# A graph layer and routed experts in one program: eight segment masks held, loads of x moved behind the edge rows, the last group's ranks and lists moved forward

## The chip, the cores and the metric

The kernel runs on one core of a Trainium2 chip. The time is device time in microseconds (us) of one execution. TensorE is PE, VectorE is DVE, ScalarE is ACT, GpSimd is POOL, SyncE is SP. "Line" is a line of the kernel before the change.

## The reference

`x` has 10000 rows of 1024 numbers (float32), and there are 5000 edges `src`, `dst`, sorted by `dst`.

```python
# 1: graph layer
h  = layernorm(x) * rsqrt(mean(square(.)) + 1e-6) * rms_w @ W_down     # 10000 x 256
xl, xr = (h @ Wl), (h @ Wr)                                            # 4 heads of 64
msg = xl[src] + xr[dst]          # edges, and one loop per row
e   = einsum(leaky(msg, 0.2), att)                                      # per head
p   = exp(e - segment_max(e, dst)[dst])
out = segment_sum(p / (segment_sum(p, dst)[dst] + 1e-16) * xl[src], dst)
x   = x + out @ W_up
# 2: experts, on xn = layernorm(x)
topk = top_k(xn @ expert_tokens.T, 2)                                   # of 8 experts
for i in range(8):
    w = mean(topk == i); y = gelu(gelu(xn @ W1[i] + b1[i]) @ W2[i] + b2[i]) @ W3[i] + b3[i]
    out2 += y * w
x = x + out2
```

A row that no edge ends in has only its loop, so its aggregate is its own `xl`; only rows that an edge ends in need the segment sums.

## The kernel before

**Engines and order.** Every engine has its own written-out program. Semaphores tie them together; nothing plans the order, it's the order of the code. SP and ACT issue plain transfers, each in its own queue, POOL the indirect ones. An issue takes the issuing engine's program time, and what stands behind it on that engine waits.

**Stage A** (0 to 403 us): 20 groups of 500 rows (125 partitions x 4 rows, `ax`). PE transposes x and multiplies by the centred `W_down` with a high and a low part of each number (`turn`, `down`), DVE makes the low parts (`low`, line 1001) and the row statistics (`bn_a`, line 973; `moments_a`), ACT the high parts. Before that, DVE scales `W_down` by `rms_w` (line 1024, 8 pieces, semaphore `wd_sums`), PE sums it over the rows (line 1650), DVE takes the mean off (line 1032), makes the low part (1040), and copies the expert tokens (`tok_c`, line 1042). Tables of `xl` and of own rows go to `node_table`.

**Stage B** (414 to 549): gathers of both ends of the edges, messages, scores, the segment maxima.

**The edge rows** (549 to 621). The edges are 40 chunks of 125, taken 4 at a time: 10 batches. DVE weighs the messages (line 1261), PE sums a carry over the chunks (line 1750), and DVE copies it (lines 1279, 1281); SP puts it as one more row below `xls` (line 449). A batch (`segment_sums`, line 1762) multiplies the weighted messages by a mask `smat` (126 x 500: same segment or not, line 1271, DVE). `finish` (lines 1284 to 1301, DVE) adds the row's own part (1293), takes the reciprocal, and scales (1299). SP stores the batch (line 455). Two masks are held: the mask of batch b + 2 is made inside `finish(b)`. The middle eight batches run in a hardware loop (`Fori`), the first and the last two are written out. ACT meanwhile weighs the own rows, and issues loads of x for the first groups of stage C (`load_cx`, line 870: 112 and 13 partitions, 2 MB together): groups 0 and 1 when the carry is copied, group 2 when the last mask is made, groups 3 to 5 when the first gather of stage C has landed.

**Stage C** (621 to 956), 20 groups: POOL gathers the aggregate (`gather_rows`, line 657), PE transposes it (line 1777), ACT splits it (`split_agg`, line 892), PE makes routing scores (1788) and eight pieces of the up projection (lines 1570 to 1572), DVE adds each to x (`residual`, 1331), takes statistics (`bn_c`), ranks the experts, and gives each row its place in a list per pair of experts: `ranks_in` and `ranks_past` on PE, `place`, `slots`, `slot_numbers` on DVE (lines 1392 to 1402), `enlist` on POOL (line 674). SP stores x1 (line 472). Six buffers `cx` hold x; from group 6 on, a load waits until the group that had its buffer is stored. For a group, ranks are counted in the group after it. For the last one they come at its end, behind the second half of its moments.

**The turn to stage R** (950 to 975): DVE computes a table of tiles from the counts (lines 1459 to 1492), SP waits for that and for all list entries, and loads lists (line 492); POOL gathers rows by them (line 714). Stage R runs 66 tiles of 256 rows, bound to a pair of experts each.

Of the kernel before, what the change touches and what calls it, by code (L numbers as in the profile page):

```python
# [23 lines left out]
HID, H = 256, 4  # L24
HD = HID // H
NE, EH = 8, 64
P, J = 125, 4
G = P * J
NG = N // G
# [8 lines left out]
CB = 4  # L38
# [17 lines left out]
NX, NI, AHEAD = 8, 16, 5  # L56
NCX = 6
NR, N3 = 4, 4
# [19 lines left out]
def build(nc, x, src, dst, rms_w, w_down, wl, wr, att, w_up, tok, w1, b1, w2, b2, w3, b3, out):  # L78
    ctx = ExitStack()
    with ctx:  # L80
# [6 lines left out]
        def run_of(at, *items):  # L87

            made = []
            for name, shape, dt in items:  # L90
                made.append(put(name, shape, dt, at))
                size = 2 if dt == BF16 else 4
                for n in shape[1:]:
                    size *= n
                at += (size + 31) // 32 * 32
            return (*made, at)

        def sem(name):
# [103 lines left out]
        tot, rden, lsb, carry, sums_end = run_of(  # L202
            at4,
            ("tot", [P, CB, H], F32), ("rden", [P, CB, H], F32), ("lsb", [NC, HV], F32), ("carry", [NC, HV], F32))
        smat, smat_end = run_of(at_wr, ("smat", [P + 1, 2, CB, P], F32))
        assert smat_end <= at_wr + 2 * KH * HID * 4

# [15 lines left out]
        xn = [xn0, xn1]  # L223
        assert c_end <= at4 - J * ROW * 4 and sums_end <= at_cx1 and edges_end + NI * NS * 4 <= at0 and xn_end <= at0, (c_end, at_cx0, edges_end, xn_end, at0)
        assert origin + max(late_end, b_end, r_end) <= nc.sbuf_usable_end, (a_end, b_end, r_end, nc.sbuf_usable_end - origin)
# [314 lines left out]
        def _(pool):  # L540
# [126 lines left out]

            def enlist(g):

                pool.wait_ge(c_slot, g + 1)  # L670
                if g == 0:
                    pool.wait_ge(sent_put, 16 * ((PAIRS + 1) * CAP // (128 * SENT)))
                for j in range(J):
                    pool.indirect_dma_start(
                        out=lists[:, :], out_offset=bass.IndirectOffsetOnAxis(ap=slot[:, g % 2, j:j + 1], axis=0),
                        in_=tok_id[:, g, j:j + 1], in_offset=None).then_inc(list_put[g % 2], 16)
# [11 lines left out]
            for g in range(NG):  # L688
# [6 lines left out]
                if g == S0 + 1:  # L695
                    lower_w2_table()
            rstd_c(NG - 1, slice(0, J // 2), NG)
            rstd_c(NG - 1, slice(J // 2, J), NG + 1)
            enlist(NG - 1)

# [47 lines left out]
        def _(act):  # L749
# [126 lines left out]
            load_cx(0)  # L876
            load_cx(1)
            with act.Fori(6, NB) as b:
                weigh_own(b)
            act.wait_ge(b_sb, NB)  # L880
            load_cx(2)
            act.wait_ge(rows_stored, 32 * NB)
            act.wait_ge(agg_loaded[0], 16 * J)
            for g in range(3, NCX):
                load_cx(g)

# [6 lines left out]

            split_agg(0)
            for g in range(NG):
                if g + 1 < NG:
                    split_agg(g + 1)
                if 2 <= g and g + NCX - 2 < NG:
                    act.wait_ge(x1_put[(g - 2) % 3], 32 * ((g - 2) // 3 + 1))
                    load_cx(g + NCX - 2)  # L900
                if g == S0:
                    act.wait_ge(raw_w2, 16 * 2)
                    act.activation(w2_tab[:, :, 0:EH], w2_raw[:, :, EH:2 * EH], ACT.Copy).then_inc(w2_hi, 1)
# [65 lines left out]
        def _(dve):  # L969
# [53 lines left out]
            for k in range(KD):  # L1023
                last = dve.tensor_scalar(wdx[:, k, 0:HID], wd_raw[:, k, :], rmsw[:, k:k + 1], None, ALU.mult)
            last.then_inc(wd_sums, 1)
            low(0)
            low(1)
            dve.wait_ge(tok_split, 1)
            dve.wait_ge(wd_sums, 2)
            for half in range(2):  # L1030
# [4 lines left out]
            for half in range(2):  # L1035
# [5 lines left out]
                                  ).then_inc(wd_ready, 1)  # L1041
            dve.tensor_copy(tok_c[:, :, :], wdx[:, :, HID:HID + NE]).then_inc(setup_v, 2)
            for piece in range(8):
                bn_a(0, piece)
# [76 lines left out]
            for i in range(NROW):  # L1121
# [18 lines left out]
                if j == J - 1 and 0 <= g - GS1 < KD:  # L1140
                    low_w1(g - GS1)
                if i == J + 1:
                    dve.wait_ge(raw_idx, 16 * 9)
                    dve.tensor_copy(idx_f[:, :, :], idx_rows[:, :, :]).then_inc(setup_v, 1)
# [122 lines left out]

            def same_segment(b, par):

                wait(dve, b_num, b - 1)  # L1270
                dve.tensor_tensor(smat[:, par, :, :],
                                  dst_row[:, bass.ds(CB * P * b, CB * P)].rearrange("p (c e) -> p c e", c=CB),
                                  dst_col[:, bass.ds(CB * b, CB)].unsqueeze(2).broadcast_to([P + 1, CB, P]),
                                  ALU.is_equal).then_inc(b_sb, 1)

            same_segment(0, 0)
            same_segment(1, 1)
            dve.wait_ge(b_l, 1)
# [4 lines left out]
            def finish(b, par):  # L1283
# [11 lines left out]
                dve.reciprocal(rden[:, :, :], tot[:, :, :]).then_inc(b_den, 1)  # L1295
                if has_batch(b, 2):
                    same_segment(b + 2, par)
                dve.wait_ge(b_den, 3 * b + 3)
                dve.tensor_tensor(by_head, by_head, rden[:, :, :].unsqueeze(3).broadcast_to([P, CB, H, HD]),
                                  ALU.mult).then_inc(b_out, 1)  # L1300

            def has_batch(b, more):
                return not isinstance(b, int) or b + more < NB

# [101 lines left out]
            for g in range(NG):  # L1406
# [35 lines left out]
                if not more:  # L1442
                    bias_c(g, slice(0, J // 2), NG)
                for u in range(6, 8):
                    residual(g, u)
                    bn_c(g, u)
                if more:
                    moments(g, g % 2, c_bn, c_aggr, c_var, 1.0, LN_EPS)
            moments(NG - 1, (NG - 1) % 2, c_bn, c_aggr, c_var, 1.0, LN_EPS, J // 2, J, 1)
            place(NG - 1)  # L1450
            slots(NG - 1)
            bias_c(NG - 1, slice(J // 2, J), NG + 1)
            slot_numbers(NG - 1)

# [112 lines left out]
        def _(pe):  # L1567
# [79 lines left out]
            pe.wait_ge(tok_split, 1)  # L1647
            pe.wait_ge(wd_sums, 1)
            for k in range(KD):
                last = pe.matmul(X_A[1][:, 0:HID + NE], ones_raw[:, :], wdx[:, k, :], start=k == 0, stop=k == KD - 1,  # L1650
                                 skip_group_check=True)
# [106 lines left out]
            def segment_sums(b, par):  # L1758
                pe.wait_ge(b_sb, b + 1)
                wait(pe, b_out, b - 1)  # L1760
                for q in range(CB):
                    last = pe.matmul(bank[4 * par + q][0:P, 0:HV], smat[:, par, q, :],
                                     xls[0:P + 1, bass.ds(CB * b + q, 1), :].rearrange("p c d -> p (c d)"),
                                     start=True, stop=True, skip_group_check=True)
                last.then_inc(b_num, 1)
# [64 lines left out]
            for g in range(NG):  # L1830
# [11 lines left out]
                if g >= 1:  # L1842
                    ranks_past(g - 1)
                for u in range(6, 8):
                    up(g, u)
            ranks_in(NG - 1)
            ranks_past(NG - 1)
# [92 lines left out]
```

## Time and profile before

| | us |
|---|---|
| three runs: median, lowest, highest | 1629.34, 1626.74, 1630.38 |
| the profiled execution's own time | 1625.11 |
| its span | 1623.4 |
| PE busy | 1486.6 (92%) |
| DVE busy | 1189.4 (73%) |
| ACT busy | 687.3 (42%) |
| POOL busy | 653.3 (40%) |

The span runs from the first to the last instruction of the profiled execution. Times of the rows further down are microseconds from its start. Busy time is a union over a stretch and can be high on several engines at once; a "<-" behind an idle time names what ended it. For a DMA the row is the issue, the landing comes later. In a row of a merged group, "x8" is the number of instructions and the length is that of the whole group.

### The profile page before, as it was taken

The numbers are of one execution on the slowest core, as the hardware profiler recorded it, in microseconds if no ns is written. First come the engines' busy times: TensorE is split into PE (matmuls) and PEld (weight loads), VectorE is DVE, ScalarE is ACT, GpSimd is POOL, SyncE is SP. The second block draws the span as 40 slices with busy tenths as digits, with TensorE's granted clock in tenths as the row PEclk, the third lists the DMA queues.
The fourth block names the chain that finished last, engine by engine and source line by source line (L and its number), as shares of the span: only waits on it lengthen the run. The fifth ranks groups of instructions, "written<-read, shape, count | busy, mean of one in ns | idle before, by whom it ended". The sixth has DMA issues, their size and how long they took to land.

```text
span 1623.4 us, 28905 instructions
## 1 busy us (share of the span) xinstructions
PE 1486.6 (92%) x9321; PEld 1234.1 (76%) x9321; DVE 1189.4 (73%) x2415; ACT 687.3 (42%) x1365; POOL 653.3 (40%) x729
## 2 busy tenths in 40 slices
PE   6999999999599654999999938999999999999997
PEld 5999999999477433888877837777777777777775
DVE  5666666667297763999999956777777777777775
ACT  2444445544244540000000005666666666566653
POOL 2112222223676002576666553444444444444432
PEclk9999999999799886999999968999999999999999
DMA  8887876552464078899999567767666666665320
GB/s 202 231 194 184 174 199 156 156 150 65 126 187 154 1 191 223 211 315 293 310 303 294 186 169 206 220 220 219 219 206 202 215 211 210 213 207 165 106 57 15
DMA packets 121662, 306.95 MB, mean 189 GB/s; under 512 B 63855, under 2 KB 65557, under 8 KB 114015
## 3 DMA queue, kind: packets, MB, share of 16 engines
q1 hardware_dynamic: 60088, 155.40, 34.8%
q0 software_dynamic: 50848, 108.78, 21.2%
q10 hardware_dynamic: 10580, 40.96, 9.8%
q8 instruction: 75, 1.23, 0.3%
q14 instruction: 71, 0.58, 0.1%
HBM read 220.40 MB, written 138.85 MB: 221 GB/s over the span
## 4 chain that ended last, share of the span: by engine, by line
PE 46%; issue 21%; DVE 17%; POOL 7%; DMA 5%; SPq 1%; ACTq 0%; POOLq 0%; DVEq 0%; ACT 0%
PE psum L1894 14%; PE psum L1862 7%; PE psum L1570 6%; PE psum L1572 5%; PE psum L1571 5%; DVE stat L973 5%; DVE cx L1331 4%; PE psum L1892 4%; POOL where_from L606 2%; POOL xls L639 1%; DVE aggt_lo L1321 1%; POOL td L643 1%; POOL rstd L595 1%; PE psum L1750 1%; DMA agg<-node_table,from_idx 1%
## 5 line engine op out<-in xcount | busy, mean ns | idle before, releaser
L1894 PE MATMUL psum<-w_raw,gl 128*128 128x512 f32 x528 | 269.7, 592 | 0.0
L917 ACT ACTIVATE xt_hi<-psum 128x512 fp32r<-128x512 f32 x264 | 151.0, 598 | 240.0 <-PE psum L1862 239.9
L1498 DVE TENSOR_TENSOR xt_lo<-psum,xt_hi 128x512 fp32r<-128x512 f32 x264 | 176.4, 689 | 87.4 <-ACT xt_hi L917 86.7
L1511 DVE SCALAR_TENSOR_TENSOR xb<-psum,xb 128x512 f32<-128x512 f32 x264 | 176.1, 687 | 28.7 <-PE psum L1894 28.6
L1609 PE MATMUL psum<-wdx_hi,axt_hi 128*125 128x272 f32 x640 | 190.7, 298 | 6.8 <-DVE wd_lo L1040 4.0
L1001 DVE TENSOR_TENSOR axt_lo<-psum,axt_hi 128x500 fp32r<-128x500 f32 x160 | 108.4, 678 | 118.2 <-ACT axt_hi L754 118.2
L1862 PEld LDWEIGHTS psum<-ident,xn 128*128 128x128 f32 x1056 | 127.1, 142 | 86.0 <-issue 68.4
L1611 PE MATMUL psum<-wdx_hi,axt_lo 128*125 128x272 f32 x640 | 184.9, 289 | 0.0
L1610 PE MATMUL psum<-wd_lo,axt_hi 128*125 128x256 f32 x640 | 179.7, 281 | 0.0
L726 POOL DMA_INDIRECT out<-xb,idx_in x132 | 134.0, 1015 | 106.2 <-issue 59.7
L911 ACT ACTIVATE xn<-xb 128x1024 f32<-128x1024 f32 x132 | 156.1, 1233 | 45.1 <-DMA xb<-rows_x,idx_in 45.1
L1570 PE MATMUL psum<-xt_hi,st_w 128*128 128x256 f32 x528 | 167.4, 317 | 0.0
L1862 PE MATMUL psum<-ident,xn 128*128 128x128 f32 x1056 | 150.3, 276 | 17.4 <-ACT xn L911 16.9
L714 POOL DMA_INDIRECT xb<-rows_x,idx_in x132 | 141.4, 1071 | 59.4 <-issue 54.7
L1892 PE MATMUL psum<-b_hl,sel_st 128*128 128x512 f32 x264 | 158.8, 601 | 0.0
L1572 PE MATMUL psum<-xt_hi,st_w 128*128 128x256 f32 x528 | 150.5, 285 | 0.0
L892 ACT ACTIVATE aggt_hi<-psum 128x500 fp32r<-128x500 f32 x40 | 21.4, 586 | 304.9 <-PE psum L1777 262.1
L1571 PE MATMUL psum<-xt_lo,st_w 128*128 128x256 f32 x528 | 150.1, 284 | 0.0
L754 ACT ACTIVATE axt_hi<-psum 128x500 fp32r<-128x500 f32 x160 | 94.3, 590 | 123.5 <-PE psum L1593 123.4
L1894 PEld LDWEIGHTS psum<-w_raw,gl 128*128 128x128 f32 x528 | 99.9, 189 | 44.1 <-issue 32.1
L1570 PE MATMUL psum<-wup_hi,aggt_hi 128*125 128x512 f32 x320 | 132.8, 415 | 0.0
L595 POOL TENSOR_TENSOR rstd<-var,neg_half 125x4 f32<-125x4 f32 x20 | 23.8, 1192 | 266.9 <-DVE var L983 266.9
(276 smaller groups left out, 3841.4 us busy)
## 6 DMA issues: line engine op xcount, KB each, us to landing
w_raw<-in_L_ffn_W SPq DMA_DIRECT2D x140, 256.0 KB, 12.5
cx<-in_x ACTq DMA_DIRECT2D x20, 1792.0 KB
rows_x<-cx SPq DMA_DIRECT2D x19, 1806.0 KB
ax<-in_x SPq DMA_DIRECT2D x19, 1792.0 KB
node_table<-trow SPq DMA_DIRECT2D x19, 896.0 KB
node_table<-xld SPq DMA_DIRECT2D x10, 448.0 KB
cx<-in_x ACTq DMA_DIRECT2D x20, 208.0 KB
rows_x<-cx SPq DMA_DIRECT2D x19, 209.6 KB
```

Source lines behind the costliest of these rows:

```text
L911: act.activation(xn[s][:, :], xb[:, b, s, 0:D], ACT.Identity, bias=xb[:, b, s, D + 1:D + 2], scale=xb[:, b, s, D:D + 1]).then_inc(r_xn, 1)
L1498: dve.tensor_tensor(xt_lo[:, 2 * q:2 * q + 2, :].rearrange("p k n -> p (k n)"), T_R[q % 2], xt_hi[:, 2 * q:2 * q + 2, :].rearrange("p k n ...
L1511: dve.scalar_tensor_tensor(piece, Y[u], 0.5, piece, ALU.mult, ALU.add).then_inc(r_res, 1)
L1570: pe.matmul(out_ap, left[0], right[0], start=start, stop=False, skip_group_check=True)
L1571: pe.matmul(out_ap, left[0], right[1], start=False, stop=False, skip_group_check=True)
L1572: return pe.matmul(out_ap, left[1], right[0], start=False, stop=stop, skip_group_check=True)
L1609: pe.matmul(into, high, wdx_hi[:, k, :], start=k == 0, stop=False, skip_group_check=True)
L1610: pe.matmul(into[:, 0:HID], high, wd_lo[:, k, :], start=False, stop=False, skip_group_check=True)
L1611: last = pe.matmul(into, low, wdx_hi[:, k, :], start=False, stop=k == KD - 1, skip_group_check=True)
L1862: last = pe.transpose(T_R[q % 2][:, TT * k + 128 * s:TT * k + 128 * (s + 1)], xn[s][:, 128 * (2 * q + k):128 * (2 * q + k + 1)], ident[:, :])
L1892: pe.matmul(Y[u], sel_st[:, t % 2, :], b3_hl[:, HALF * n:HALF * (n + 1)], start=True, stop=False, skip_group_check=True)
L1894: pe.matmul(Y[u], gl2[:, t % 2, rows], w3_raw[:, t % N3, HALF * n:HALF * (n + 1)], start=False, stop=True, skip_group_check=True).then_inc ...
```

## The change

- `smat` holds eight masks (`NSM`) in place of two. It moves to the place that the small sums had, and these to the place of the masks. Eight masks are made before the carry's copy; `finish` makes one only in the written-out batches 0 and 1 (for 8 and 9).
- `load_cx`: group 0 as before, group 1 when the edge rows are stored and the first gather has landed, groups 2 to 5 behind the first `split_agg`.
- Start: the wait for the scaled weights is split in two (`wd_sums`); four of eight statistics pieces of group 0 stand ahead of the wait for the sums; the copy `tok_c` moves to the fifth row step of stage A.
- Last group: PE counts the ranks between its up pieces 6 and 7, DVE makes the slots ahead of residuals 6 and 7, POOL issues two list entries ahead of the last power and two behind.

```diff
-NCX = 6
+NCX, NSM = 6, 8
...
-            at4,
+            at_wr,
             ("tot", [P, CB, H], F32), ("rden", [P, CB, H], F32), ("lsb", [NC, HV], F32), ("carry", [NC, HV], F32))
-        smat, smat_end = run_of(at_wr, ("smat", [P + 1, 2, CB, P], F32))
+        smat, smat_end = run_of(at4, ("smat", [P + 1, NSM, CB, P], F32))
...
-            def enlist(g):
+            def enlist(g, first=0, past=J):
...
-                for j in range(J):
+                for j in range(first, past):
...
             rstd_c(NG - 1, slice(0, J // 2), NG)
+            enlist(NG - 1, 0, J // 2)
             rstd_c(NG - 1, slice(J // 2, J), NG + 1)
-            enlist(NG - 1)
+            enlist(NG - 1, J // 2, J)
...
             load_cx(0)
-            load_cx(1)
             with act.Fori(6, NB) as b:
                 weigh_own(b)
-            act.wait_ge(b_sb, NB)
-            load_cx(2)
             act.wait_ge(rows_stored, 32 * NB)
             act.wait_ge(agg_loaded[0], 16 * J)
-            for g in range(3, NCX):
-                load_cx(g)
+            load_cx(1)
...
             split_agg(0)
+            for g in range(2, NCX):
+                load_cx(g)
...
-            last.then_inc(wd_sums, 1)
+                if k % (KD // 2) == KD // 2 - 1:
+                    last.then_inc(wd_sums, 1)
             low(0)
             low(1)
+            for piece in range(4):
+                bn_a(0, piece)
             dve.wait_ge(tok_split, 1)
-            dve.wait_ge(wd_sums, 2)
+            dve.wait_ge(wd_sums, 3)
...
-            dve.tensor_copy(tok_c[:, :, :], wdx[:, :, HID:HID + NE]).then_inc(setup_v, 2)
-            for piece in range(8):
+            for piece in range(4, 8):
                 bn_a(0, piece)
...
+                if i == J:
+                    dve.tensor_copy(tok_c[:, :, :], wdx[:, :, HID:HID + NE]).then_inc(setup_v, 2)
...
-            same_segment(0, 0)
-            same_segment(1, 1)
+            for b in range(NSM):
+                same_segment(b)
...
-                if has_batch(b, 2):
-                    same_segment(b + 2, par)
+                if isinstance(b, int) and b + NSM < NB:
+                    same_segment(b + NSM)
...
                 if not more:
                     bias_c(g, slice(0, J // 2), NG)
+                if not more:
+                    place(g)
+                    slots(g)
+                    slot_numbers(g)
...
             moments(NG - 1, (NG - 1) % 2, c_bn, c_aggr, c_var, 1.0, LN_EPS, J // 2, J, 1)
-            place(NG - 1)
-            slots(NG - 1)
             bias_c(NG - 1, slice(J // 2, J), NG + 1)
-            slot_numbers(NG - 1)
...
-            pe.wait_ge(wd_sums, 1)
             for k in range(KD):
+                if k % (KD // 2) == 0:
+                    pe.wait_ge(wd_sums, 2 * k // KD + 1)
...
-                for u in range(6, 8):
-                    up(g, u)
-            ranks_in(NG - 1)
+                if g == NG - 1:
+                    up(g, 6)
+                    ranks_in(g)
+                    up(g, 7)
+                else:
+                    for u in range(6, 8):
+                        up(g, u)
             ranks_past(NG - 1)
```

## Rows read from the trace of the kernel before

**Rows 1.** Busy time by stretch: engine busy (count), granted PE clock, DMA share, GB/s.

```profile
60.00:500.00 440.00, 417.13 (x3366) 401.27 (x3366) 288.00 (x639) 199.78 (x433) 140.60 (x161) 0.98 0.64 163
...
640.00:660.00 20.00, 20.00 (x97) 16.49 (x96) 16.80 (x39) 1.07 (x2) 2.17 (x2) 0.93 1.00 221
...
700.00:1050.00 350.00, 316.03 (x1695) 258.20 (x1694) 301.03 (x717) 66.14 (x111) 198.30 (x195) 0.94 0.84 253
...
1100.00:1600.00 500.00, 500.00 (x2872) 375.64 (x2871) 374.11 (x629) 307.92 (x524) 213.84 (x247) 1.00 0.59 180
```

**Rows 2.** Timeline of the start: start, length, what, idle time before.

```profile
11.77 5.11 PE L1650 MATMUL psum<-wdx,ones_raw 128*128 128x264 f32 x16
...
17.00 2.42 DVE L1032 SCALAR_TENSOR_TENSOR wdx<-psum,wdx 128x1056 f32<-128x1056 f32 x2 [3.69 <-PE psum L1650]
...
21.90 1.27 DVE L1042 COPY tok_c<-wdx 128x64 f32<-128x64 f32 x1
...
23.09 4.83 DVE L973 BATCH_NORM_STATS2 stat<-ax 125x6 f32<-125x512 f32 x8
...
25.89 0.59 PE L1593 MATMUL psum<-ident,ax 125*128 125x125 f32 x4
...
29.33 0.39 PE L1609 MATMUL psum<-wdx_hi,axt_hi 128*125 128x272 f32 x1 [2.84 <-DVE axt_lo L1001]
```

**Rows 3.** Timeline of the edge rows, DVE, and PE's first batch.

```profile
570.22 0.42 DVE L1279 COPY lsb<-psum 40x260 f32<-40x260 f32 x1 [7.83 <-PE psum L1750]
...
590.15 0.17 DVE L1290 SCALAR_TENSOR_TENSOR tot<-psum,pexp 125x16 f32<-125x16 f32 x1
...
591.53 0.62 DVE L1271 TENSOR_TENSOR smat<-dst_row,dst_col 126x500 f32 x1
...
593.19 0.17 DVE L1290 SCALAR_TENSOR_TENSOR tot<-psum,pexp 125x16 f32<-125x16 f32 x1
...
608.39 0.17 DVE L1290 SCALAR_TENSOR_TENSOR tot<-psum,pexp 125x16 f32<-125x16 f32 x1
...
611.04 0.17 DVE L1290 SCALAR_TENSOR_TENSOR tot<-psum,pexp 125x16 f32<-125x16 f32 x1
...
580.20 5.93 PE L1762 MATMUL psum<-xls,smat 126*125 126x260 f32 x16 [8.87 <-DMA xls<-carry]
```

**Rows 4.** Chain at the last store; DMA busy strip of 595 to 605.

```profile
614.50 6.51 DMA node_table<-xld
...
DMA  9986310008999876200006999888300009999988
```

**Rows 5.** Chain and ACT timeline at the start of stage C.

```profile
629.97 0.62 ACTq L870
...
634.02 0.60 ACT aggt_hi L892
...
647.13 1.07 ACT L892 ACTIVATE aggt_hi<-psum 128x500 fp32r<-128x500 f32 x2 [12.04 <-PE psum L1777]
```

**Rows 6.** SyncE's DMA issues at 13 to 14 us.

```profile
13.11 7.83 SPq L411 DMA_DIRECT2D b_raw<-in_L_ffn_b  x1
```

**Rows 7.** Gathers of stage C (line 657), and PE's waits of 640 to 945.

```profile
DMA to landing us min/median/max: 2.8/8.9/15.0
...
PE psum L1777 <- DMA agg<-node_table,from_idx: 3.9, 4, 1.7
```

**Rows 8.** Timeline of the last group: DVE, then POOL, then SyncE.

```profile
949.09 0.42 DVE L1392 TENSOR_TENSOR steps<-psum,onehot 125x256 f32<-125x256 f32 x1
...
950.56 0.23 DVE L1459 TENSOR_TENSOR beats<-psum,bcap 125x64 f32<-125x64 f32 x1 [0.32 <-PE psum L1806]
...
955.27 0.42 DVE L1492 CAST tile_tab<-psum 1x264 int32<-1x264 f32 x1 [1.09 <-PE psum L1852]
...
955.70 1.18 POOL L674 DMA_INDIRECT lists<-tok_id,slot  x1 [0.30 <-issue]
...
959.31 4.75 SPq L492 DMA_DIRECT2D idx_in<-lists  x5
```

More of the change, by code:

```diff
@@ L202, in build @@
         tot, rden, lsb, carry, sums_end = run_of(
-            at4,
+            at_wr,
             ("tot", [P, CB, H], F32), ("rden", [P, CB, H], F32), ("lsb", [NC, HV], F32), ("carry", [NC, HV], F32))
-        smat, smat_end = run_of(at_wr, ("smat", [P + 1, 2, CB, P], F32))
-        assert smat_end <= at_wr + 2 * KH * HID * 4
+        smat, smat_end = run_of(at4, ("smat", [P + 1, NSM, CB, P], F32))
+        assert sums_end <= at_wr + 2 * KH * HID * 4
         cx3, cx4, agg, aggt_hi, aggt_lo, cx5, c_end = run_of(
@@ L223, in build @@
         xn = [xn0, xn1]
-        assert c_end <= at4 - J * ROW * 4 and sums_end <= at_cx1 and edges_end + NI * NS * 4 <= at0 and xn_end <= at0, (c_end, at_cx0, edges_end, xn_end, at0)
+        assert c_end <= at4 - J * ROW * 4 and smat_end <= at_cx0 and edges_end + NI * NS * 4 <= at0 and xn_end <= at0, (c_end, at_cx0, edges_end, xn_end, at0)
         assert origin + max(late_end, b_end, r_end) <= nc.sbuf_usable_end, (a_end, b_end, r_end, nc.sbuf_usable_end - origin)
@@ L1266, in _, with same_segment @@
                 weigh(b)
[L1268 to L1273, printed above, removed]
+            def same_segment(b):
+                dve.tensor_tensor(smat[:, b % NSM, :, :],
+                                  dst_row[:, CB * P * b:CB * P * (b + 1)].rearrange("p (c e) -> p c e", c=CB),
+                                  dst_col[:, CB * b:CB * (b + 1)].unsqueeze(2).broadcast_to([P + 1, CB, P]),
                                   ALU.is_equal).then_inc(b_sb, 1)
-            same_segment(0, 0)
-            same_segment(1, 1)
+            for b in range(NSM):
+                same_segment(b)
             dve.wait_ge(b_l, 1)
@@ L1300, in finish @@
                                   ALU.mult).then_inc(b_out, 1)
-            def has_batch(b, more):
-                return not isinstance(b, int) or b + more < NB
             for par in range(2):
@@ L1761, in segment_sums @@
                 for q in range(CB):
-                    last = pe.matmul(bank[4 * par + q][0:P, 0:HV], smat[:, par, q, :],
+                    last = pe.matmul(bank[4 * par + q][0:P, 0:HV], smat[:, b % NSM, q, :],
                                      xls[0:P + 1, bass.ds(CB * b + q, 1), :].rearrange("p c d -> p (c d)"),
```

## The prediction

> **What bounds the kernel now.** Every term below is measured against the profiled execution, whose own time is 1625.1 us around a span of 1623.4 us (the table of times above); the median of the three timed runs is 1629.3, which is 4.2 us above it. I read the table of stretches first, then the timeline at the two ends of each stage, then the chain of waits.
>
> The stretches [rows 1] show two long stages in which TensorE (PE) does the work and one in which it shares the bound. The first stage (normalise and project all rows, "stage A") keeps PE at 417 of 440 us, and most of what is missing there lies at its far end. The last one (the experts, "stage R") keeps PE at 500 of 500. Between 700 and 1050, mostly the 20 row groups of "stage C" (aggregate, up projection, residual, routing), VectorE (DVE) is busy for 301 us and PE for 316 of 350. The change touches none of the loops of A and R in number or kind of instruction. So it can only move the joints: the first 30 us, the edge rows at 584 to 634, and the turn from C to R at 945 to 960. The order of work inside a long stage is fixed, and whatever a joint gives is carried to the end, unless the next stage waits for something that didn't move.
>
> **1. The start.** PE goes through the sums over the weights without a wait before them: that row has no idle time noted [rows 2]. The new split of the wait (first half, then all) therefore removes nothing: 0, and bounded by 0 on both sides within rounding.
>
> Moving the first four statistics pieces of group 0 ahead of the wait for those sums is another matter. DVE stands idle for 3.69 us until 17.00 for PE's sums; four pieces cost 4 x 0.60 = 2.4 us (4.83 us for eight) and fit in, if their rows have landed. The rows of that group are loaded in four parts in order, PE has used the first by 12, and there is room of 1.3 us. Behind the centred weights, DVE now runs the copy of the tokens (21.90, 1.27 us; its next instruction starts 1.19 later), eight pieces (4.83 us), then the moments, and only then the low part for which PE waits: 2.84 us idle until 29.33 [rows 2]. Without the copy and with four pieces fewer, DVE reaches that low part 1.2 + 2.4 = 3.6 us earlier, at 25.0. PE itself ends its transposes only at 26.48 (25.89 + 0.59), so of the 3.6 no more than the 2.84 of idle time can go: the next step of PE starts at about 26.4. What is late next is the load of group 1: DVE's first piece of it stood behind the low part, at 29.2, and now comes at about 26; by the order and size of the loads it may have to wait until 27.5, which puts the second low part some 0.4 us behind its old distance. I take **2.5 us**, between 0 (the load of group 1 sets the pace anyway) and 2.84.
>
> The copy of the tokens comes back later in stage A (1.27 us, once), where DVE has 152 of 440 us free [rows 1] and PE is fed from four buffers: 0, at most 1.3 if it hits a low part directly.
>
> **2. The edge rows.** Ten batches run on DVE one after the other. A batch with a mask made inside takes 3.04 us (590.15 to 593.19), the last one, which makes none, 2.65 (608.39 to 611.04) [rows 3]. Now eight masks are made ahead, and only batches 0 and 1 still make one (for 8 and 9), so batches 2 to 7 go from 3.04 to 2.65: 6 x 0.39 = **2.3 us**. The six additional masks, of 0.62 us each, lie before the copy at 570.22, ahead of which DVE idles 7.83 us: 3.7 us of masks are hidden, with 4 to spare. What could be late next is PE: it needs 2.0 us for a batch's sums and may begin one when DVE has finished two batches before, so it has 2.65 us and is still hidden by some 0.4. Bounds: 0 (PE or the register arithmetic of the loop is exposed) to 6 x 0.62 = 3.7, the whole mask.
>
> **3. The last stores of the edge rows.** Before the gathers of stage C may start, all stores must have landed. The last one takes 6.51 us from its issue [rows 4], because the load of x for group 2 was released by the last mask at 607 and lies in front and among the stores. With nothing beside them, stores show as separate bursts in the strip of 595 to 605 (a digit is 0.25 us): issued every 3.04 us, the bursts end some 2.9 us behind the issue and the queues fall idle between them. The change moves that load behind the gathers, so the last store should take about 3.0: **3.5 us**, between 0 and 3.9. The earlier load of group 1 is moved too. It ended beside the first stores, with no wait depending on it, 0. The load of group 0 is still issued beside the carry row, so PE's wait of 8.87 us for that row [rows 3] stays; I give the missing second load nothing there, since it queued behind the first (bounds 0 to 4).
>
> **4. ScalarE's issues ahead of the first high part.** When the first gather has landed, ScalarE (ACT) issues six halves of loads, then splits the aggregate: the third issue starts at 629.97 and the split at 634.02 [rows 5]. Now only the load of group 1 (two issues) stands there. So the split starts where the third issue did: **4.0 us**. The other eight issues come behind the split. They take 0.6 to 0.9 us each, 6 to 8 us together, and behind them waits the split of group 1. That was due 13.1 us after the first (647.13), with 12.04 us idle before it [rows 5]: cover for 5 to 6 us more.
>
> This is the weakest place. Never were more than three loads (6 MB) in flight on ACT's queue; now it's five, 10 MB. And on SyncE's queue, one issue took 7.83 us in place of 0.3 to 0.4 when much was in flight [rows 6]. The Trainium skill, page "DMA: Bandwidth & Descriptors", section "Anatomy of one DMA", says of GpSimd's path that descriptor generation is a small part of a transfer's fixed cost and that many can be emitted before it shows; by that rule the eight issues stay cheap and the sum stands, by the row just named they may not.
>
> Do the loads come in time? Loads alone run at 221 GB/s (640 to 660, DMA share 1.00 [rows 1]), so 2 MB take 9.3 us. Group 1's x lands some 10 us behind the split and is used 24 behind it; those of 2 to 5 land by 22, 31, 40 and 50 and are used at 39, 54, 70 and 85. No residual waits for x.
>
> **5. The last group.** Now the ranks of group 19 are counted and turned into slots ahead of its residuals 6 and 7, and the first half of the list entries goes out before the last moments. Three small DVE steps (0.42, 0.42, 0.17 with their waits: 1.1 us, [rows 8]) move ahead of the last two residuals, so those, the second moments, the last bias (949.99) and the last store come 1.1 us later; the count of tiles starts 0.65 later than 950.56, since it no longer follows the slots but the bias. The tile table is then written at 955.9 instead of 955.27, done by 956.4. On GpSimd (POOL), the last four list issues, 1.49 us apart, end with the one at 955.70; its landing, about 2.6 us later at 958.3, lets SyncE read two numbers and issue the first list at 959.31, 1.0 behind [rows 8]. Two of the four now run at 947 to 950, beside the residuals; the two others start behind the second power at 951.2, the last at 952.7, so that they land 2.5 us later at 955.3. The gate is no longer the lists but the tile table at 956.4, against 958.3: **1.9 us**, between 0 (the stores of x1, later by 1.1, become the gate) and 2.9 (the lists alone).
>
> **Sum:** 2.5 + 2.3 + 3.5 + 4.0 + 1.9 = 14.2 us. The profiled execution would go from 1625.1 to 1610.9, the median of runs from 1629.3 to **1615**.
>
> **The rivals.**
>
> *ACT's queue holds no more than three loads.* For it speaks the 7.83 us issue [rows 6]; against it, that the six issues at 628 to 634 show no such wait, and that SyncE's slow one was of another shape. Price: the fourth load is let in when group 1's has landed and the fifth when group 2's has, about 22 us behind the first split (two loads of 9.3 us and the gathers between them). The split of group 1, due at 13, is 9 us late, and with it PE and DVE. Gain 14.2 - 9 = 5: **1624**.
>
> *The start gives nothing that lasts.* The load of group 1, or the table's and the map's stores between A and the gathers at 414, set the pace and not PE. The map's last writes follow a power of DVE's last moments, which PE paces, which speaks against. Gain 11.7: **1617.6**.
>
> *DMA is the bound of stage C.* Two loads, 4.1 MB, are moved from the edge rows, where the queues were partly idle, into the stage where the DMA share is 0.84 on average at 253 GB/s [rows 1]. If nothing there is spare, they cost 4.1 / 0.253 = 16 us and eat the rest: **1631**, no change. Against it: DVE waits in C for no load, only for PE.
>
> *The gathers come late (the other side, slower).* A gather of a group lands 2.8 to 15.0 us behind its issue, median 8.9, and is used about 15 us after it; PE already waits for it four times, 3.9 us in all, 1.7 at most [rows 7]. With more loads queued for longer, the gathers of groups 3 to 19 would each come 1.7 us late and DVE, the bound, would follow: 17 x 1.7 = 29 us, **1644**. It decides from 14.2 / 17 = 0.84 us per group. The Trainium skill, same page, section "Queues, rings and completion order", says that an engine goes round-robin between its queues packet by packet; by that a longer queue of loads takes no more from the gathers than a short one that is never empty. In the rows, the share stays high through C before the change too, which agrees but doesn't settle the first 40 us.
>
> **How the numbers follow.** Forecast 0.62, ACT's queue 0.18, start lost 0.09, DMA bound 0.05, gathers late 0.06. A difference under 0.2% (3.3 us) can't be told from none. Faster: the forecast, the lost start, and three quarters of the queue's case (it gains 5, less if the wait is longer): 0.84. Same: the rest of that case and the DMA bound, 0.09. Slower: 0.07. For the range: all upper bounds together, 2.84 + 3.7 + 3.9 + 4 (carry row) + 4.0 + 2.9 = 21.3, would give 1608, which is unlikely as a whole; the low end is 1610. The high end takes in the queue's case: 1625.
>
> **What would show it.** In the profile after: PE's wait at 29.33 gone and its step at 26.4 to 27; tot instructions 2.65 us apart from the third batch on; the first gather of stage C 6 us closer to the first batch; the first split of the aggregate 1.5 us behind the first gather's landing and not 5.6; the eight issues behind it under 1 us each, and the second split still 13 us after the first; groups of C still 15.3 us apart; the first list read about 2 us closer to the last residual. It would be wrong if an issue among the eight takes several us, if residuals wait for x, or if stage C takes longer than before from its first split to its last.

## The result and the profile after

| | before, us | after, us |
|---|---|---|
| median of 12 runs each | 1627.99 | 1622.32 |
| lowest, highest | 1621.65, 1634.11 | 1615.82, 1624.68 |
| profiled execution: own time, span | 1625.11, 1623.4 | 1623.03, 1621.3 |

The ratio is 0.996, with a 95% interval of 0.9944 to 0.9977. The change makes the kernel faster by 0.4%, 5.7 us by the medians. Forecast were 14.2 us and a time of 1615; the measured one lies in the range (1610 to 1625) only by its upper part, which had been drawn for the rival "ACT's queue holds no more than three loads" (1624). The gain itself is less than half of the one forecast.

The stretches of the kernel after come first, in the columns of [rows 1] (the five busy times are those of PE, PE's weight loads, DVE, ACT and POOL):

```profile
60.00:500.00 440.00, 417.21 (x3358) 400.38 (x3358) 288.91 (x641) 199.22 (x434) 142.72 (x162) 0.98 0.65 164
640.00:660.00 20.00, 11.54 (x44) 9.65 (x43) 9.96 (x26) 1.06 (x2) 4.93 (x5) 0.66 1.04 215
700.00:1050.00 350.00, 313.85 (x1695) 255.39 (x1696) 301.34 (x717) 66.35 (x111) 197.54 (x196) 0.95 0.85 254
1100.00:1600.00 500.00, 500.00 (x2876) 375.84 (x2875) 374.68 (x628) 306.93 (x523) 214.01 (x247) 1.00 0.58 179
```

The long stages are as they were. The odd row is the second: PE worked for 20 of the 20 us before [rows 1], and now for 11.54, with the DMA share still full. That hole is new, and the timeline of ScalarE and its queue shows what made it (start, length, what, idle time before and its cause; ACTq is ACT issuing a DMA):

```profile
619.78 1.62 ACTq L871 DMA_DIRECT2D cx<-in_x  x2
621.45 0.59 ACT L889 ACTIVATE aggt_hi<-psum 128x500 fp32r<-128x500 f32 x1 [33.86 <-PE psum L1778]
...
623.67 3.36 ACTq L871 DMA_DIRECT2D cx<-in_x  x1
...
628.17 8.62 ACTq L871 DMA_DIRECT2D cx<-in_x  x1
...
638.48 7.83 ACTq L871 DMA_DIRECT2D cx<-in_x  x1
...
646.37 1.06 ACT L889 ACTIVATE aggt_hi<-psum 128x500 fp32r<-128x500 f32 x2 [23.85 <-issue]
```

The first split stands at 621.45, where it was 634.02 [rows 5]. Then come the eight issues. Three of them don't take 0.6 to 0.9 us but 3.36, 8.62 and 7.83 (all three are the second, small issue of a load, that of 13 partitions), and the second split waits behind them: "23.85 <-issue" says that it waited for nothing but its own engine's issues. It starts 24.92 us after the first; before, the distance was 13.11 [rows 5]. The first split had been 12.57 us sooner than before; of these, 11.81 are gone at the second. DVE and PE pass the wait on (their rows at the second group):

```profile
646.99 0.68 DVE L1320 TENSOR_TENSOR aggt_lo<-psum,aggt_hi 128x500 fp32r<-128x500 f32 x1 [8.77 <-ACT aggt_hi L889]
...
649.24 0.38 PE L1789 MATMUL psum<-m,aggt_hi 128*125 128x16 f32 x1 [8.46 <-DVE aggt_lo L1320]
```

Both traces cut at the same landmarks give the account. "C" is stage C, and "last scaling" is the end of DVE's last one.

| from, to | before | after | gained |
|---|---|---|---|
| start to first gather of stage B | 414.59 | 413.42 | 1.17 |
| to PE's first edge sums | 165.61 | 164.19 | 1.42 |
| first edge sums to last scaling | 33.57 | 31.15 | 2.42 |
| last scaling to first gather of C | 8.02 | 4.11 | 3.91 |
| first gather to first split | 12.24 | 8.59 | 3.65 |
| first split to second split | 13.11 | 24.92 | -11.81 |
| second to last (20th) split | 275.75 | 277.38 | -1.63 |
| last split to first list load | 36.35 | 35.00 | 1.35 |
| first list load to end | 664.17 | 662.55 | 1.62 |
| sum (the spans) | 1623.41 | 1621.31 | 2.10 |

How far can such a row be read? The same landmarks in the nine profiles of before, after and the versions below (all but e4) say it. The second row took 163.4 to 168.0 us and the seventh 275.8 to 279.3 (once 283.6), with the same instructions in them. The first row is 414.4 to 415.0 in the three with the old start, but 412.2 to 416.1 in the six with the new one. The last row took 662.1 to 664.4. So 1.17, 1.42, -1.63 and 1.62 are no findings of their own. The rows from the edge sums to the first split repeat to 0.6 us at most.

The rows at the start, to be set against [rows 2]:

```profile
11.81 5.89 PE L1651 MATMUL psum<-wdx,ones_raw 128*128 128x264 f32 x16
17.82 2.42 DVE L1034 SCALAR_TENSOR_TENSOR wdx<-psum,wdx 128x1056 f32<-128x1056 f32 x2 [2.09 <-PE psum L1651]
...
22.71 2.47 DVE L972 BATCH_NORM_STATS2 stat<-ax 125x6 f32<-125x512 f32 x4
25.32 0.42 DVE L979 BATCH_NORM_AGGREGATE mv<-stat 125x2 f32<-125x12 f32 x4
25.78 0.17 DVE L982 TENSOR_SCALAR var<-mv 125x4 f32<-125x4 f32 x1
25.86 0.67 DVE L1000 TENSOR_TENSOR axt_lo<-psum,axt_hi 128x500 fp32r<-128x500 f32 x1
27.18 0.69 DVE L972 BATCH_NORM_STATS2 stat<-ax 125x6 f32<-125x512 f32 x1 [0.65 <-DMA ax<-in_x]
```

Only four pieces are left behind the weights (2.47 us, 4.83 before), and DVE's low part comes at 25.86 instead of 28.60. The last row is what is late next, as forecast: the load of group 1. One thing ate into the gain in this execution: PE's weight sums ended 0.8 later (17.70, against 16.88), and all behind them with it.

The edge rows (DVE; against [rows 3]) and the last store (against [rows 4]):

```profile
558.83 4.79 DVE L1273 TENSOR_TENSOR smat<-dst_row,dst_col 126x500 f32<-126x500 int32 x8
568.17 0.42 DVE L1281 COPY lsb<-psum 40x260 f32<-40x260 f32 x1 [4.54 <-PE psum L1751]
...
577.60 6.32 PE L1763 MATMUL psum<-xls,smat 126*125 126x260 f32 x16 [8.33 <-DMA xls<-carry]
...
587.56 0.17 DVE L1292 SCALAR_TENSOR_TENSOR tot<-psum,pexp 125x16 f32<-125x16 f32 x1
...
590.20 0.17 DVE L1292 SCALAR_TENSOR_TENSOR tot<-psum,pexp 125x16 f32<-125x16 f32 x1
...
607.53 1.23 DVE L1301 TENSOR_TENSOR xld<-xld,rden 125x1024 f32<-125x1024 f32 x1
612.15 0.24 DVE L1315 MEMSET cx<- 125x24 f32 x6 [3.40 <-DMA node_table<-xld]
612.86 0.95 POOL L657 DMA_INDIRECT agg<-node_table,from_idx  x1 [91.30 <-DMA node_table<-xld]
```

Eight masks take 4.79 us ahead of the copy, and DVE still idles 4.54 before it. Batches are 2.64 apart from the third on. DVE waits 3.40 us for the last store.

The last group (DVE, POOL, SyncE; against [rows 8]):

```profile
945.96 0.14 DVE L1340 SCALAR_TENSOR_TENSOR cx<-mv,cx 125x2 f32<-125x2 f32 x1
946.02 0.41 DVE L1391 TENSOR_TENSOR steps<-psum,onehot 125x256 f32<-125x256 f32 x1
...
948.03 1.24 POOL L674 DMA_INDIRECT lists<-tok_id,slot  x1 [3.55 <-DVE slot L1401]
...
953.32 1.18 POOL L674 DMA_INDIRECT lists<-tok_id,slot  x1 [0.30 <-issue]
956.02 0.42 DVE L1492 CAST tile_tab<-psum 1x264 int32<-1x264 f32 x1 [1.08 <-PE psum L1857]
957.53 0.48 DVE L1533 MEMSET st_w<- 128x512 f32 x1 [1.09 <-DMA rows_x<-cx]
...
958.84 2.60 SPq L492 DMA_DIRECT2D idx_in<-lists  x3
```

The order is the new one. The forecast's times were on the clock of the profile before, where the last split stands at 922.88; here it stands at 923.75, so distances from it are what can be compared. The tile table comes 32.3 us behind it (32.4 before, 33.0 forecast) and the last list entry goes out 29.6 behind it (29.8 forecast). But the first list is read 35.0 behind it by the table above and not 34.5 as forecast (36.35 before): the last list entry went out at 953.32 and took 4.44 us to land,

```profile
953.32 4.44 DMA lists<-tok_id,slot
```

beside the last store of x1, which DVE's row at 957.53 also waits for. In all seven profiles with the new order that entry takes 4.1 to 4.4 us and goes out 1.2 us behind the last store of x1; in the three with the old order it takes 2.5 to 2.6 and goes out 5.2 behind. The gate stayed the lists.

### The profile page after: what moved, and what is told of

It is laid out like the page before. It is cut to its first block and busy times, and to the rows that moved or that the text cites. A ratio compares the mean times of both kernels' runs of the same rounds, so it can differ in the third digit from the quotient of the medians.

```text
span 1621.3 us, 28896 instructions
## 1 busy us (share of the span) xinstructions
PE 1488.0 (92%) x9321; PEld 1234.7 (76%) x9321; DVE 1189.9 (73%) x2415; ACT 686.2 (42%) x1365; POOL 653.3 (40%) x729
## 3 DMA queue, kind: packets, MB, share of 16 engines
q10 hardware_dynamic: 10580, 40.96, 10.0%
```

## The experiments

All are ratios to the kernel before, run on the same chip, with 95% intervals. The question of the first four: do the long issues take back what the moved loads give (theory Q), or is DMA the bound of stage C (rival D), and what are the start and the last group worth alone?

**e1_spread.** The kernel after, with two loads behind the first split and one behind each of the next two, instead of four behind the first:

```diff
-            for g in range(2, NCX):
+            for g in range(2, NCX - 2):
                 load_cx(g)
 ...
-                if 2 <= g and g + NCX - 2 < NG:
-                    act.wait_ge(x1_put[(g - 2) % 3], 32 * ((g - 2) // 3 + 1))
+                if g + NCX - 2 < NG:
+                    if g >= 2:
+                        act.wait_ge(x1_put[(g - 2) % 3], 32 * ((g - 2) // 3 + 1))
                     load_cx(g + NCX - 2)
```

> The changed kernel, but only the loads of groups 2 and 3 stand behind the first split; the load of group 4 is issued behind the second split and that of group 5 behind the third. Rival D (stage C pays for the moved bytes anyway, the blocked issue is only where it shows): the second split is early, but the groups behind it are late by as much, and the ratio stays near 0.996.

Measured: 1613.47 us (before 1626.27), ratio 0.9926, 0.99 to 0.9952; repeated as e8_spread_again below: 1612.34, ratio 0.9914, 0.9891 to 0.9936. ACT in the first of them:

```profile
620.19 0.59 ACT L889 ACTIVATE aggt_hi<-psum 128x500 fp32r<-128x500 f32 x1 [34.30 <-PE psum L1779]
...
622.41 2.61 ACTq L871 DMA_DIRECT2D cx<-in_x  x1
633.33 0.59 ACT L889 ACTIVATE aggt_hi<-psum 128x500 fp32r<-128x500 f32 x1 [12.08 <-PE psum L1779]
633.76 0.61 ACTq L871 DMA_DIRECT2D cx<-in_x  x1
```

The same loads in the same number, and the second split is back at 13.14 us, again with 12.08 us of idle time waiting for PE. One issue is still long (2.61), inside that cover. The DMA share of 615 to 645 is even higher than in the kernel after, as the two stretches (after, then e1) show, and PE does more:

```profile
615.00:645.00 30.00, 19.41 (x81) 16.14 (x81) 9.27 (x20) 1.06 (x2) 9.51 (x11) 0.73 0.89 210
```

```profile
615.00:645.00 30.00, 24.89 (x117) 21.33 (x118) 17.23 (x41) 2.13 (x4) 9.77 (x11) 0.77 0.92 223
```

So the order of the issues lost the time and not the amount of DMA. That the blocked issues cost the 12 us is shown, and rival D, which had the ratio stay near 0.996, has fallen in both series. The ratio expected was 0.989, which this series just misses and its repetition holds; one row shows a small part of what rival D said. ACT has one step in stage C that waits for a load of expert weights, and the sixth split stands behind it:

```profile
697.41 0.58 ACT L903 ACTIVATE w_tab<-w_raw 128x448 fp32r<-128x448 f32 x1 [17.39 <-DMA w_raw<-in_L_ffn_W]
```

In the four profiles with spread loads (this one, e6, e7, e8) the second half of these weights lands 33.6 to 35.2 us behind its issue, in those of before, after, e2, e3 and e5 19.7 to 21.5. The sixth split comes 19.0 to 20.5 us behind the fifth and not 14.6 to 15.3, and PE then waits 0.5 us (here), 1.3 (e8), 1.6 (e7) and 3.9 (e6), where it waits 0.4 at most at a time in the five others. So the spread order seems to have a small price of its own; no run moved the weights' load alone, so that the spread loads are what delays it isn't shown.

**e2_start.** The kernel before with the change's start alone (four statistics pieces ahead, the split wait, `tok_c` moved).

> Before, with the start alone changed (split wait, four statistics pieces forward, token copy later). From the prediction 2.5 us less, ratio 0.9985. From the profile after (the gathers of stage B began 1.2 us earlier, with the sums over the weights 0.8 us longer) 1 to 2 us, ratio 0.999. Rival: nothing of it lasts, 1.000.

Measured: 1623.37 us, ratio 0.9982, 0.997 to 0.9993: 2.9 us less, between 1.1 and 4.9. In its profile the first gather of stage B starts at 412.18 against 414.59, 2.4 sooner, in a row that spreads by 4 us over the profiles with the new start. Something of the start's gain reaches the end of stage A; how much, the time says only within that interval.

**e3_end.** The kernel before with the last group's new order alone (PE's ranks between pieces 6 and 7, slots ahead of the residuals, lists two and two).

> Before, with the last group alone changed (ranks, slots and two list issues ahead of the last residuals). The prediction says 1.9 us less, ratio 0.9988; the profile after says 0.7 us, since the last lists land 4.5 us after their issue beside the later store of x1, ratio 0.9996. Rival: the later stores of x1 are the gate and it's 0 to 1 us slower.

Measured: 1625.18 us, ratio 0.9988, 0.9976 to 1.0. The interval touches 1. The traces say more: from the last split to the first list load, the three profiles with the old order show 36.35, 35.66 and 36.51 us, the six with the new order 34.22 to 35.65, mean 34.8. By the means it's worth 1.3 us, though the nearest two of the nine touch (35.66 and 35.65).

**e4_half.** The kernel after with each load of x issued as two loads of half rows: the same bytes in twice as many descriptors of half the size.

```diff
-                    act.dma_start(cx[g % NCX][rows, :, 0:D],
-                                  x_g[g, rows, :].rearrange("p (j d) -> p j d", j=J)).then_inc(cx_loaded[g % NCX], 16)
+                    for n in range(2):
+                        act.dma_start(cx[g % NCX][rows, :, HALF * n:HALF * (n + 1)],
+                                      x_g[g, rows, :].rearrange("p (j d) -> p j d", j=J)[:, :, HALF * n:HALF * (n + 1)]
+                                      ).then_inc(cx_loaded[g % NCX], 16)
```

> The changed kernel, with each load of x issued as two half rows: same bytes, twice the descriptors (2 KB in place of 4 KB) and twice the issues. Theory Q by descriptors: all but about 90 of 340 descriptors per ring must be done before ACT is free, about 7.5 of 10 MB in place of 4.8, so the second split comes some 38 us after the first in place of 24.9, and the time is 12 to 16 us above the changed kernel. Rival B, the queue is limited by bytes: the second split stays at about 25 us plus some 6 us for the additional issues where nothing blocks. Rival I, by the number of DMAs in flight (about 5): blocked after the first load, later still.

Measured: 1633.48 us, ratio 1.0045, 1.003 to 1.006: 7 us slower than the kernel before and, by the two ratios, 14 slower than the kernel after. ACT and its queue:

```profile
619.33 0.59 ACT L891 ACTIVATE aggt_hi<-psum 128x500 fp32r<-128x500 f32 x1 [31.98 <-issue]
...
620.71 4.06 ACTq L872 DMA_DIRECT2D cx<-in_x  x1
...
626.33 5.02 ACTq L872 DMA_DIRECT2D cx<-in_x  x1
...
656.52 1.07 ACT L891 ACTIVATE aggt_hi<-psum 128x500 fp32r<-128x500 f32 x2 [36.13 <-issue]
```

The second split is 37.2 us behind the first. In the kernel after, the first long issue comes when three large and two small issues, 5.9 MB, are out; here it comes after four large and two small halves, 3.9 MB. The queue's packets are 21160 against 10580 for 40.96 MB. What was issued less what the packet records show as moved gives what was open when the first long issue ended, as a mean over 16 rings: 79 packets (4.8 MB in all) in the kernel after, 84 packets (2.6 MB) here. So what fills up goes by descriptors and not by bytes, and rival B has fallen. Rival I (the number of DMAs in flight) doesn't fit either: the sixth issue of the stage is the long one of the kernel after, and the sixth here takes 0.64 us, each with none of the five before it complete. The count itself isn't one number: the later long issues ended at 85 to 87 open packets in the kernel after and at 95 to 125 here. What sets it stays open.

The second four runs ask what the parts are worth, and whether the carry row can be helped.

**e5_loads.** The kernel before with the new load order alone (two masks, old start and end).

> The kernel before with only the new order of x loads (group 0 at the carry row, group 1 when the first gather has landed, groups 2 to 5 behind the first split; two masks, old start and end). Theory Q (the long issues of the loads take back what the moved loads give): +3.5 for the last store's landing, +4.0 for the two loads less ahead of the first split, -11.8 for the second split, -1.6 for the rest of stage C, so about 6 us slower than the kernel before: ratio 1.003 to 1.005; an issue of 3 us and two of 8 us behind the first split, second split 24 to 25 us after the first. Rival (the order of loads gives 7.5 us and the long issues are absorbed by slack later in stage C): ratio 0.995 to 0.998.

Measured: 1630.15 us (before 1625.86), ratio 1.0022, 1.0005 to 1.0039: the loads' new order alone makes the kernel slower, by 3.5 us (0.8 to 6.3), less than the 0.3 to 0.5% expected. From the last scaling to the first gather 4.10 us, to the first split 8.55, to the second split 23.40: 3.9 and 3.7 gained, 10.3 lost. That alone is -2.7; the forecast of -6 had taken 11.8 and the 1.6 us of noise of stage C as well. The rival (absorbed) has fallen. The two gains don't hang on the masks: they are the same with two and with eight (3.9 and 3.65). The loss is 1.5 us smaller here, which has no row to explain it.

**e6_two_masks.** The spread version with two masks made inside the batches, all else the same.

> The spread version with two masks made inside the batches in place of eight held: every other part the same. Theory (a mask inside a batch costs 0.39 us, six of them are gone): 2.4 us slower than the spread version, batches 3.04 us apart, no other stage changed; ratio to the kernel before about 0.994 where the spread version has 0.9925. Rival M (the six masks ahead of the first sums delay the copy for the carry row and PE's first sums, so that the gain is lost): no difference between the two versions, with PE's first sums earlier here.

Measured: 1618.22 us, ratio 0.9942, 0.9922 to 0.9963, against 1612.34 for the version with eight on the same chip. The medians differ in the direction forecast, but the two intervals overlap a little, so the time alone doesn't show it; the size of 2.4 lies inside them. By the trace, the stretch from the first batch to the last scaling's end is 29.70 instead of 27.28 us, 2.42 more, and batches stand 3.04 apart. DVE idles 7.91 us before the carry's copy with two masks and still 4.63 with eight, and PE's first sums follow that copy by 8.44 and 8.21 us: the six masks ahead delay nothing, rival M has fallen. Stage C took 283.64 us in this profile, 4.4 more than in e8, and that lies between the first split and the seventh: 96.1 us against 91.6. There the expert weights of the row shown under e1 landed at 703.49, and PE waited 3.9 us behind the sixth split. How much of the 5.9 between the medians is such a wait, single profiles can't say.

**e7_carry_alone.** The spread version with group 0's load behind ACT's last own products:

```diff
-            load_cx(0)
             with act.Fori(6, NB) as b:
                 weigh_own(b)
+            load_cx(0)
```

> The spread version with group 0's load of x issued behind ScalarE's last own products (about 587 us) and no longer together with the store of the carry row. Theory C (the carry row waits in the queues behind the 2 MB load): PE's wait for it of 8.3 us falls to 3 to 4 us, the edge rows begin 4 to 5 us sooner and the whole span is as much shorter, ratio to the kernel before 0.9895 to 0.990, and the first stores, beside which the load now runs, land late without harm. Rival L (the load now lies among the stores and the last of them lands late): the first gather of stage C comes 3 to 4 us later behind the last scaling, gain 0 to 1 us. Rival K (the 8.3 us are the carry row's own latency, 125 partitions or not): the wait stays over 7 us, gain 0.

Measured: 1610.2 us, ratio 0.9893, 0.9871 to 0.9915, beside 1612.34 for the spread version. PE's wait and the last store:

```profile
578.07 0.85 SPq L449 DMA_DIRECT2D xls<-carry  x1
581.49 5.23 PE L1764 MATMUL psum<-xls,smat 126*125 126x260 f32 x16 [3.90 <-DMA xls<-carry]
...
591.10 0.72 ACTq L871 DMA_DIRECT2D cx<-in_x  x1
...
615.66 0.24 DVE L1316 MEMSET cx<- 125x24 f32 x6 [3.39 <-DMA node_table<-xld]
```

The wait falls from 8.25 us to 3.90, and the last store still lands 3.39 behind its scaling. Theory C is right in its mechanism, rivals L and K have fallen. The two medians are 2.1 us apart, less than the 4.35 that the row gained, and the intervals overlap; so the gain in time isn't shown by itself. In this profile it can't be seen in the span (1613.7) either: from the first gather of B to PE's first sums it took 165.4 us with the wait 4.35 shorter, where the spread version's two profiles took 164.0 and 164.2. It is the fastest version by median and beats both kernels.

**e8_spread_again.** The spread version, for the same chip.

> The spread version once more, so that the two above stand beside it on the same chip: ratio to the kernel before 0.990 to 0.995, as in its first series (0.9926).

Measured: 1612.34, ratio 0.9914 (0.9891 to 0.9936). Beside 0.9926, it shows how well a series repeats: 0.1%.

## Why the prediction was right and where it was not

Of the forecast's sum of 14.2 us the five terms named came within 0.6 us each, and one that it left at zero, the blocked issues, was the largest of all. The forecast itself, 1615, missed by 7 us; that the time fell into the range is owed to the range's upper end, which took this rival in at a chance of 0.18.

1. **The start**: 2.5 forecast; 2.9 in time (1.1 to 4.9) when done alone (e2). In the profiles the low part comes 2.5 to 4.5 us sooner (24.1 to 25.9 against 28.4 to 28.7), and the first gather of stage B 1.0 sooner by the means of six profiles and three, with a spread of 4. The time shows the sign, and 2.5 lies in its interval; the side remark on group 1's load by the row at 27.18.
2. **The edge rows**: 2.3 forecast, 2.42 measured, and the same 2.42 when they are taken out again (e6). Batch distance 2.64 (forecast 2.65), masks hidden (4.5 us left, forecast 4). The two outer bounds (0, 3.7) were not needed.
3. **The last stores**: 3.5 forecast, 3.9 measured in the kernel after and in e5. A store with nothing beside it lands about 3.4 us after DVE is done. The upper bound was the truth.
4. **Issues ahead of the first split**: 4.0 forecast, 3.65 measured. But the step "they take 0.6 to 0.9 us each, 6 to 8 us together" failed: the eight took 25 us, of which three took 19.8, and -11.8 us stood where the prediction had 0. The prediction called it the weakest place and named the cause as a rival, with 9 us as its price and 0.18 as its chance. The mechanism was this one; the price came out 2.8 us short: the last issue was let in and done 24.9 us behind the first split, where the rival had 22. The chance was too low. The argument against it, "the six issues at 628 to 634 show no such wait", was read too kindly: six issues are three loads, 1587 packets (10580 for 20 loads), 99 for each of 16 rings, of which some 93 were open when the sixth began and 86 when it ended. That is just what fits, and the sixth had taken 1.74 us already, twice the usual time of 0.9. The Trainium skill, page "DMA: Bandwidth & Descriptors", section "Anatomy of one DMA", says of GpSimd's path that many descriptors can be emitted before the added cost shows. The prediction carried that over to ACT's queue, and there the rows at 623.67 to 646.3 disagree.
5. **The last group**: 1.9 forecast, 1.3 measured over nine profiles. The step that let the last list entry land 2.6 us behind its issue was mis-sized: it took 4.44 us, beside the store of x1. The lists stayed the gate and the tile table didn't become it.

The sum with the terms measured is 2.9 + 2.4 + 3.9 + 3.65 + 1.3 - 11.8 = 2.4 us (0.7 with the start's 1.2 of that profile); the two profiles differ by 2.1. The parts timed alone give 2.9 (e2) - 3.5 (e5) + 1.9 (e3) + 2.4 (masks) = 3.7. By the medians of the change it's 5.7, with an interval of 3.7 to 9.1. The intervals of the parts cover the difference, but its 2 to 3 us have no row, and they stay open; single executions of one kernel differ by 9 to 12 us. Without the block, the terms make 14.2, and the spread version is 12.8 and 13.5 us faster than before in its two series. So the forecast's gain was there for a kernel with its issues in another order.

Of the other rivals: "the start gives nothing that lasts" fell with e2; "DMA is the bound of stage C" fell with e1, which moves the same bytes at a higher share (what is left of it is the late expert weights there); "the gathers come late" did not happen, PE waits for gathers 5.1 us in stage C (3.9 before [rows 7]) and never longer than 2.0.

## What to carry to other kernels

An issue of a DMA is an instruction of its engine and can block it, here for up to 8.62 us, and with it all that stands behind it. Before moving loads in front of an engine's next compute step, count what is open on its queue at that moment, in descriptors and not in bytes. Put loads that aren't needed soon behind the steps that are, one by one; four loads in one block behind the first split cost 11.8 us, and with two there and one behind each of the next two splits the second split comes 13.1 to 14.1 us behind the first again (13.1 before). Then look further down for what comes late beside the moved traffic, as the expert weights here. And if the profile shows a queue at work without a wait, look whether its last issue is already longer than the others (1.74 us against 0.9 in the kernel before): here the room ended just there.

## What the runs showed that was not expected

- A small DMA beside a large one pays by waiting: the carry row (41.6 KB) took 8.2 to 8.6 us from the start of its copy to PE's first sums with one 2 MB load issued at the same moment, 8.5 to 8.8 with two of them, and 3.87 us with none (e7). In e4, where the one load came in half rows, it took 7.2.
- Loads in pieces of half a row cost the transfers little, 10.7% of the DMA engines' span for that queue and not 10.0%, but the issues much: fifteen took 36.4 us.
- Stage B, with the same instructions, took 163.4 to 168.0 us up to the first sums from profile to profile, and 169.8 in e7 with its 4.4 us of shorter wait put back. The cause was not looked for.
